# A graph network's row gathers: part of them issued row by row by SyncE and ScalarE instead of GpSimd

## The chip, the cores and the metric

The kernel runs on one core of a Trainium2 chip. The core has five engines with queues of their own: TensorE (PE, with its weight loads as PEld), VectorE (DVE), ScalarE (ACT), GpSimd (POOL) and SyncE (SP), and 16 DMA engines that all of them use. The metric is the time of one execution on the device, in microseconds (us).

## The reference, cut to what matters

Two graph layers on 12500 nodes of 128 numbers and 400000 edges sorted by destination. The change touches the first, a relational layer that is applied twice. Its core is a gather, a scaling and a sum by destination:

```
h   = relu(layernorm(x))
rel = argmax(edge_attr[:, 16:26])                  # relation of each edge, 0..9
seg = dst * 10 + rel
mean[seg] = sum over its edges of h[src] / count(seg)
h   = relu(einsum('nrd,rdo->no', mean, w_rel1) + h @ root1 + b1)
y   = the same once more with w_rel2, root2, b2;  x = x + y
```

The second layer is graph attention (xl[src], xr[dst], a softmax over the edges of a node, a weighted sum of xl[src]); the change leaves it alone.

## The kernel before, in words

The relational layer is turned round: for every node n and relation r the product h[n] @ w_rel[r] is made first and stored in DRAM as a table (`ytab` for the first pass, `ytab2` for the second). It has a row of 128 floats, 512 bytes, for each of the keys src*10 + rel. A pass then fetches for every edge the row of its key, scales it by 1/count, and sums rows by destination.

The 400000 edges are 3125 tiles of 128. Five tiles are a group (G = 5), five groups are a round (SLOTS = 5), so a pass has 625 groups and 125 rounds. I call the work on one group a slot.

- GpSimd (`gather_engine`) issues one indirect DMA a tile (L714), which fetches 128 rows by 128 keys. Five buffers `p_g` of a group each and five key buffers `p_i` go round. Before it refills one it waits until ScalarE has scaled the group five slots back (`s_free`, which is `s_v`).
- ScalarE (`rgcn_pass`) waits for the gather of a group, copies the keys of the group five slots ahead into `p_i` (L755), reads one number from a table into a register (`load`, L114), and scales the five tiles into a ring `p_v` of ten groups (L761).
- VectorE builds a 0/1 matrix from the destinations (L616) and adds each product to the node sums `A` (L635). TensorE multiplies the two (L678), five products a step.
- From group 500 or so on, the same loops also make the next table, node tile by node tile: for the second pass in pass 1 (`NextTable`), the attention's `xlw` and `xrw` in pass 2 (`Attention`). SyncE moves those tiles (its `sync` methods). Until then SyncE has nothing to do in a pass.

The prologue makes keys, counts and the first table. What sets the order is written out by hand: each engine has its own program, and semaphores tie them together.

In a row of the profile, L114 stands for the helper `load`, which reads numbers from SBUF into registers (TENSOR_LOAD), and L110 for the helper `gate`, which waits. Tile names lose their pass number: `p_g` is p1_g or p2_g.

Of the kernel before, what the change touches and what calls it, by code (L numbers as in the profile page):

```python
# [20 lines left out]
I32 = mybir.dt.int32  # L21
ALU = mybir.AluOpType
ACT = mybir.ActivationFunctionType
AX = mybir.AxisListType.X
ds = bass.ds

P = 128
N = 12500
D = 128
# [8 lines left out]
G = 5  # L38
# [18 lines left out]
LOOK = 6  # L57
ROUNDS = GROUPS // SLOTS
# [25 lines left out]
assert all(BLOCK * (NBLK - 2) + OUT_AT[b] >= GROUPS + OB * b + OB - 1 for b in range(OUTS))  # L84
assert AHEAD == UNROLL and NT % 2 == 0 and STEPS + UNROLL <= SCOLS * P
# [3 lines left out]
def build(nc, x, src, dst, attr, w_rel1, root1, b1, w_rel2, root2, b2, w_l, w_r, att, bias, out,  # L89
# [3 lines left out]
    def sem(name):  # L93
        return outer.enter_context(nc.semaphore(name))
# [50 lines left out]
    src_dram = nc.dram_tensor("src_dram", (P, CE), I32, kind="Internal").ap()  # L145
    xjw = nc.dram_tensor("xjw", (GROUPS + 1, P, GW), F32, kind="Internal").ap()

    with outer:
# [20 lines left out]
        def prologue():  # L169

            with ExitStack() as st:
# [24 lines left out]
                junk = rel_all[:, 0:GROUPS]  # L196
                ones = sbuf(st, "ones", [1, P])
# [23 lines left out]
                s_ea = [sem(f"ea_in{k}") for k in range(2)]  # L221
                s_dst, s_src, s_nb = sem("dst_in"), sem("src_in"), sem("neighbours_in")
                s_last, s_rel, s_iota = sem("last_in"), sem("ea_used"), sem("iotas")
                s_const, s_raw = sem("prep_const"), sem("raw_free")
                s_tp, s_ev = sem("turned"), sem("to_turn")
                s_pa, s_tz, s_key = sem("psum_free_act"), sem("turned_early"), sem("keys")
                s_tw, s_inv, s_wa = sem("turned_weights"), sem("inverse_counts"), sem("weights_copied")
                s_tab, s_step = sem("tables_made"), sem("tables_moved")
                s_eps, s_w = sem("t1_eps_set"), sem("t1_w_in")
                s_x = [sem(f"t1_x_in{k}") for k in range(2)]  # L230
                s_st, s_var, s_std, s_rs = sem("t1_stats"), sem("t1_variance"), sem("t1_std"), sem("t1_rstd")
                s_hn, s_t, s_ht = sem("t1_rows"), sem("t1_turned"), sem("t1_copied")
                s_m0, s_m1, s_y0, s_y1 = sem("t1_product0"), sem("t1_product1"), sem("t1_out0"), sem("t1_out1")
                s_out = [sem(f"t1_stored{k}") for k in range(2)]
                NB = NT // BT

                with nc.Block() as block:

                    @block.sync
                    def _(sp):  # L240
# [28 lines left out]
                        sp.dma_start(base[:, :], base_dram.rearrange("(a s) -> a s", a=1).to_broadcast([P, SCOLS * P])).then_inc(s_step, 16)  # L269
                        for k in range(2):  # L270
                            sp.wait_ge(s_out[k], 16 * (NT // 2))
                        sp.dma_start(steps[:, :], step_dram[0].rearrange("(a s) k -> a (s k)", a=1)).then_inc(s_step, 16)
                        sp.wait_ge(s_step, 192)
# [14 lines left out]
                    def _(dve):  # L288
# [111 lines left out]
                        v.engine_nop().then_inc(s_key, 1)  # L400
                        link(v.memset(tot, 1.0))
# [194 lines left out]
        def sum_engines(block, name, onehot, colsp, pg, V, width, s_v, s_pe, s_acc, then, localise=False):  # L596

            s_dl, s_oh = sem(f"{name}_local"), sem(f"{name}_onehot")
            s_cp = sem(f"{name}_cols_set")
# [100 lines left out]
        def gather_engine(block, rows, stage, gbuf, s_stage, s_g, s_free, s_kept=None):  # L700

            @block.gpsimd
            def _(pool):
                def round_(i, peel):
                    for k in range(SLOTS):
                        if peel:
                            pool.wait_ge(s_stage, k + 1)
                        else:

                            gate(pool, "pool", (s_free, SLOTS * (i - 1) + k + 1))  # L710
                            if s_kept is not None:
                                gate(pool, "pool", (s_kept[k], 16 * i))
# [999 lines left out]
```

## Time and profile before

| | us |
|---|---|
| runs on the device, median of 3 (lowest, highest) | 12650.64 (12648.94, 12654.09) |
| profiled execution: its own time is its span | 12683.4 |
| prologue, 0 to 680 | 680 |
| pass 1, first to last gather | 3907.5 |
| between the passes | 37 |
| pass 2, first to last gather | 3908 |
| change-over and attention | 4150 |

Busy shares over the whole span (the page's first part): PE 57%, DVE 42%, ACT 33%, POOL 71%. These are averages over stages that differ, so the stage of the two passes has to be read by itself. [...]

### The profile page before, as it was taken

To read this page: it belongs to the slowest core of one execution; us is meant where nothing else is said; L and a number is where in the kernel's file an instruction comes from. 1 tells how busy PE (TensorE), PEld (TensorE's weight loads), DVE (VectorE), ACT (ScalarE), POOL (GpSimd) and SP (SyncE) were. 2 spreads that over 40 slices of the span, in tenths; PEclk is the share of its full clock that TensorE was granted. 3 is DMA by queue.
4 is the path that set the end of the run, shared out by engine and by line. 5 is a ranking of instruction groups with operands and counts; after the bars stand their busy time and mean duration, and the time that the engine had idled before them with its cause. 6 is when DMAs were issued, how large, how long until landed. Compare 5 with 4: busy or idle time off the path is not lost. (4 is left out here: it accounts for less than half of the span.)

```text
span 12683.4 us, 185431 instructions
## 1 busy us (share of the span) xinstructions
PE 7179.3 (57%) x34895; PEld 6004.9 (47%) x34896; DVE 5378.0 (42%) x11674; ACT 4188.5 (33%) x12473; POOL 9042.4 (71%) x9581
## 2 busy tenths in 40 slices
PE   3744444444444864444444444556777877777777
PEld 1333333333333543333333343444666766666666
DVE  7832222222222641111111111353776766776767
ACT  2522222222222222222222222223444444444442
POOL 0167777777777767777777777767777777777776
PEclk8855555555555975555555555667998898998988
DMA  8622221122122542111222122236888888888887
GB/s 239 204 59 52 52 52 53 52 53 52 53 52 59 185 137 53 52 53 52 53 52 53 52 53 52 73 88 172 236 237 234 237 236 236 235 236 235 236 235 207
DMA packets 922670, 1589.56 MB, mean 125 GB/s; under 512 B 303128, under 2 KB 487318, under 8 KB 915334
## 3 DMA queue, kind: packets, MB, share of 16 engines
q0 software_dynamic: 314112, 685.63, 21.9%
q1 hardware_dynamic: 384568, 595.99, 15.3%
q10 hardware_dynamic: 223412, 301.41, 7.7%
q8 instruction: 219, 3.59, 0.1%
q14 instruction: 359, 2.94, 0.1%
HBM read 1213.18 MB, written 367.39 MB: 125 GB/s over the span
## 5 line engine op out<-in xcount | busy, mean ns | idle before, releaser
L714 POOL DMA_INDIRECT p_g<-ytab,p_i x6250 | 5912.3, 946 | 1973.2 <-issue 1661.9
L1165 POOL DMA_INDIRECT a_g<-xlw,a_i x3125 | 2986.1, 956 | 995.5 <-issue 875.4
L678 PE MATMUL p_pg<-p_v,p_oh 128*128 x6120 | 1338.9, 397 | 1550.0 <-ACT p_v L761 1549.4
L761 ACT ACTIVATE p_v<-p_g,wgt_all 128x128 f32<-128x128 f32 x6250 | 1960.4, 389 | 542.1 <-issue 517.0
L678 PEld LDWEIGHTS p_pg<-p_v,p_oh 128*128 128x128 f32 x6120 | 1200.0, 295 | 1710.1 <-issue 1699.5
L755 ACT ACTIVATE p_i<-rel_all 128x5 int32 (+1 forms) x1250 | 260.0, 208 | 5065.5 <-DMA p_g<-ytab,p_i 5065.5
L678 PE MATMUL p_pt<-p_v,p_oh 128*128 x4200 | 978.1, 416 | 1277.7 <-ACT p_v L761 1277.7
L678 PEld LDWEIGHTS p_pt<-p_v,p_oh 128*128 128x128 f32 x4200 | 876.4, 313 | 1376.5 <-issue 1376.5
L616 DVE TENSOR_TENSOR p_oh<-p_cols,local 128x640 f32<-128x640 f32 x1460 | 1196.1, 820 | 24.9
L1636 PE MATMUL a_px<-a_g,ident 128*128 x1450 | 740.7, 597 | 761.7 <-SPq L1219 673.0
L1625 PE MATMUL a_pg<-a_v,a_into 128*128 128x132 f32 x7000 | 984.2, 291 | 121.2 <-DVE A L1550 43.8
L635 DVE TENSOR_TENSOR A<-p_pg,A 128x128 f32 x612 | 178.0, 291 | 1978.6 <-PE p_pg L678 1977.3
L1625 PEld LDWEIGHTS a_pg<-a_v,a_into 128*128 128x128 f32 x7000 | 910.6, 203 | 139.2 <-issue 95.7
L1268 ACT ACTIVATE a_away<-a_dst,a_minus 128x640 f32 x727 | 602.8, 829 | 970.8 <-issue 385.3
L678 PE MATMUL y_py<-p_v,p_oh 128*128 x2080 | 494.2, 423 | 649.8 <-ACT p_v L761 649.8
L635 DVE TENSOR_TENSOR A<-p_pt,A 128x128 f32 x420 | 122.6, 292 | 1677.3 <-PE p_pt L678 1677.2
L1321 ACT ACTIVATE a_relu<-a_px 128x384 f32<-128x384 f32 x725 | 351.9, 485 | 1300.5 <-PE a_py L1642 1270.6
L678 PEld LDWEIGHTS y_py<-p_v,p_oh 128*128 128x128 f32 x2080 | 441.6, 318 | 700.2 <-issue 699.5
L1642 PEld LDWEIGHTS a_px<-a_xr,a_onto 128*128 128x128 f32 x4350 | 708.9, 220 | 69.0
L1642 PE MATMUL a_px<-a_xr,a_onto 128*128 128x132 f32 x4350 | 705.4, 306 | 0.0
L1559 DVE TENSOR_TENSOR a_relu<-a_relu,a_pcon 128x640 f32<-128x640 f32 x725 | 587.9, 811 | 274.1 <-ACT a_relu L1322 273.2
L1636 PEld LDWEIGHTS a_px<-a_g,ident 128*128 128x128 f32 x1450 | 243.0, 210 | 839.7 <-issue 838.6
(254 smaller groups left out, 9818.0 us busy)
## 6 DMA issues: line engine op xcount, KB each, us to landing
a_xj<-xjw ACTq DMA_DIRECT2D x725, 330.0 KB
xjw<-a_g SPq DMA_DIRECT2D x625, 330.0 KB
a_dst<-in_dst_dram SPq DMA_DIRECT2D x625, 320.0 KB
p_g<-ytab,p_i POOLq DMA_INDIRECT x6250
ytab<-steps POOLq DMA_DIRECT2D x98, 640.0 KB, 3.6
ytab<-src_i SPq DMA_DIRECT2D x98, 640.0 KB
ea<-in_edge_attr_dram SPq DMA_DIRECT2D x50, 1176.0 KB
a_g<-xlw,a_i POOLq DMA_INDIRECT x3125
```

The costliest lines, as they stand in the source:

```text
L616: v.tensor_tensor(onehot[k][:, :].rearrange("p (t n) -> p t n", t=G), colsp[:, 0:P].rearrange("p (a n) -> p a n", a=1).to_broadcast([P, G, ...
L635: v.tensor_tensor(A[:, ds(to[k], width)], pg[b][:, 0:width], A[:, ds(to[k], width)], ALU.add).then_inc(s_acc, 1)
L678: last = t.matmul(pg[b][:, 0:width], onehot[(at + k) % LOOK][:, q * P:(q + 1) * P], V[:, ds(to + q * width, width)], start=(q == 0), stop= ...
L714: pool.indirect_dma_start(gbuf[k][:, q * D:(q + 1) * D], None, rows, bass.IndirectOffsetOnAxis(ap=stage[k][:, q:q + 1], axis=0)).then_inc( ...
L761: last = a.activation(V[:, c:c + D], gbuf[k][:, q * D:(q + 1) * D], ACT.Copy, scale=wgt[:, ds(G * g + q, 1)])
L1165: pool.indirect_dma_start(gbuf[k][:, q * W:(q + 1) * W], None, xlw, bass.IndirectOffsetOnAxis(ap=stage[k][:, q:q + 1], axis=0)).then_inc(s ...
L1268: a.activation(away[:, :], dall[:, ds(at, GE)], ACT.Abs, bias=minus[:, ds(s, 1)]).then_inc(s_away, 1)
L1321: a.activation(lk[:, 0:HEADT, :], x3[:, :, 0:D], ACT.Relu)
L1559: v.tensor_tensor(lk, lk, attp.rearrange("p (a d) -> p a d", a=1).to_broadcast([P, G, D]), ALU.mult).then_inc(s_wt, 1)
L1625: last = t.matmul(sums(j, b), into[b][:, q * P:(q + 1) * P], V[b][:, q * W:(q + 1) * W], start=(q == 0), stop=(q == G - 1))
L1636: t.matmul(px[b], ident[:, :], gath[:, ds(ring, HEADT * W)], start=True, stop=False)
L1642: last = t.matmul(to, onto[b][:, q * P:(q + 1) * P], xr[k % RING][:, :], start=False, stop=q in (HEADT - 1, G - 1))
```

## The change

In each turn of ten rounds, the last tile of the last group of a round is no longer fetched by GpSimd in nine of the ten rounds. SyncE fetches it in rounds 1, 3, 5, 6 and 8 of turns 0 to 9, ScalarE in rounds 2, 4, 7 and 9 of all turns (12.5 turns a pass; the last has rounds 0 to 4). That is 50 + 50 tiles a pass, 200 of 6250 in all.

Such a tile is fetched as 128 transfers of one row. The keys, times 512, are made once in the prologue (`row_keys`). The engine fetches a line of 128 of them to SBUF, reads them into registers (16 at a time on SyncE, 4 on ScalarE), and issues one DMA of 512 bytes for each into a row of its own buffer (`p_spr`, `p_acr`), five and four buffers. ScalarE does so in pieces of four rows (I call one a chunk), 64 chunks in each five rounds, spread over the first 22 of their 25 slots, up to three after the scaling of a slot. SyncE does whole tiles, one after the other. When the tile is due, ScalarE waits for its 128 rows and scales them in place of the gathered ones.

Besides, the gather loop and ScalarE's loop now hold ten rounds in their bodies (before: one and two), and the semaphores of a phase are cleared and freed at its end, with a barrier of all engines (`clear_spent`, three times). A part of what SyncE did at the start of `sync` is now called ahead of its tiles (`sync_first`).

```
+TURN = 10
+FULL_TURNS = 10
+SP_ROUNDS = (1, 3, 5, 6, 8)
+ACT_ROUNDS = (2, 4, 7, 9)
+SP_BUFS, ACT_BUFS = 5, 4
+ROW = D * 4
+KEYS = (NT * P * NREL - 1) * ROW
+LOADED = 16
...
+ACT_SHARES = [[] for _ in range(TURN * SLOTS)]
+for _h in range(2):
+    _own = [m for m in range(len(ACT_ROUNDS)) if TURN // 2 * _h <= ACT_ROUNDS[m] < TURN // 2 * (_h + 1)]
+    _parts = [(m, c) for m in _own for c in range(0, P, 4)]
+    for _i, _part in enumerate(_parts):
+        ACT_SHARES[TURN // 2 * SLOTS * _h + _i * 22 // len(_parts)].append(_part)
...
+    def clear_spent():
+
+        nc.clear_and_free_semaphores(list(spent))
+        spent.clear()
+        nc.all_engine_barrier()
 
...
+                        sp.dma_start(row_keys, rk[:, :]).then_inc(s_step, 16)
...
+                        v.tensor_scalar(rk[:, :], key[:, CE - P:CE], float(ROW), None, ALU.mult).then_inc(s_rk, 1)
...
+        def by_rows(turn, r):
+
+            full = not isinstance(turn, int) or turn < FULL_TURNS
+            if full and r in SP_ROUNDS:
+                m = SP_ROUNDS.index(r)
+                return "sp", m % SP_BUFS, len(SP_ROUNDS) // SP_BUFS * turn + (m // SP_BUFS + 1)
+            if r in ACT_ROUNDS:
+                m = ACT_ROUNDS.index(r)
+                return "act", m % ACT_BUFS, len(ACT_ROUNDS) // ACT_BUFS * turn + (m // ACT_BUFS + 1)
+            return None
+
...
+        def gather_engine(block, rows, stage, gbuf, s_stage, s_g, s_free):
 
             @block.gpsimd
...
+                def body(turn):
+                    for r in range(rounds_in(turn)):
+                        for k in range(SLOTS):
+                            if isinstance(turn, int) and turn == 0 and r == 0:
+                                pool.wait_ge(s_stage, k + 1)
+                            else:
+
+                                gate(pool, "pool", (s_free, TURN * SLOTS * turn + (SLOTS * (r - 1) + k + 1)))
+                            for q in range(G):
+                                if k == SLOTS - 1 and q == G - 1 and by_rows(turn, r) is not None:
+                                    continue
+                                pool.indirect_dma_start(
+                                    gbuf[k][:, q * D:(q + 1) * D], None, rows,
...
+                        def keys(turn, m):
+
+                            sp.dma_start(spidx[m % SP_BUFS][:, :], row_keys[ds(TURN * turn + SP_ROUNDS[m], 1), :]).then_inc(s_spi[m % SP_BUFS], 16)
+
+                        def tile(turn, m, again):
+                            b, n = m % SP_BUFS, len(SP_ROUNDS)
+                            fills = n // SP_BUFS
+                            gate(sp, "sp", (s_spi[b], 16 * fills * turn + 16 * (m // SP_BUFS + 1)))
+                            if m >= SP_BUFS:
+                                gate(sp, "sp", (s_v, TURN * SLOTS * turn + SLOTS * (SP_ROUNDS[m - SP_BUFS] + 1)))
+                            elif not (isinstance(turn, int) and turn == 0):
+                                gate(sp, "sp", (s_v, TURN * SLOTS * turn + SLOTS * (SP_ROUNDS[m - SP_BUFS] + 1 - TURN)))
+                            for c in range(0, P, LOADED):
+                                at = load(sp, SP_, spidx[b], c, LOADED, KEYS)
+                                for e in range(LOADED):
+                                    sp.dma_start(sprow[b][c + e:c + e + 1, :].bitcast(U8),
+                                                 octets[ds(at[e], ROW)].rearrange("(a d) -> a d", a=1)).then_inc(s_spr[b], 16)
+                            if m + SP_BUFS < n:
+                                keys(turn, m + SP_BUFS)
+                            elif again:
+                                keys(turn + 1, m + SP_BUFS - n)
...
+                        then.sync_first(sp)
+                        for m in range(SP_BUFS):
+                            keys(0, m)
+                        for m in range(len(SP_ROUNDS)):
+                            tile(0, m, True)
+                        with sp.Fori(1, FULL_TURNS - 1) as turn:
+                            for m in range(len(SP_ROUNDS)):
+                                tile(turn, m, True)
+                        for m in range(len(SP_ROUNDS)):
+                            tile(FULL_TURNS - 1, m, False)
                         then.sync(sp)
 
                     @block.scalar
...
+                        def some_rows(turn, m, c):
+
+                            b = m % ACT_BUFS
+                            if c == 0:
+                                gate(act, "act", (s_aci[b], 16 * fills * turn + 16 * (m // ACT_BUFS + 1)))
+                                if m >= ACT_BUFS:
+                                    gate(act, "act", (s_v, TURN * SLOTS * turn + SLOTS * (ACT_ROUNDS[m - ACT_BUFS] + 1)))
+                                elif not (isinstance(turn, int) and turn == 0):
+                                    gate(act, "act", (s_v, TURN * SLOTS * turn + SLOTS * (ACT_ROUNDS[m - ACT_BUFS] + 1 - TURN)))
+                            at = load(act, ACT_, actidx[b], c, 4, KEYS)
+                            for e in range(4):
+                                act.dma_start(actrow[b][c + e:c + e + 1, :].bitcast(U8),
+                                              octets[ds(at[e], ROW)].rearrange("(a d) -> a d", a=1)).then_inc(s_acr[b], 16)
+                            if c + 4 == P:
+                                if m + ACT_BUFS < n:
+                                    if not (isinstance(turn, int) and TURN * turn + ACT_ROUNDS[m + ACT_BUFS] >= ROUNDS):
+                                        keys(turn, m + ACT_BUFS)
+                                elif not (isinstance(turn, int) and TURN * (turn + 1) + ACT_ROUNDS[m + ACT_BUFS - n] >= ROUNDS):
+                                    keys(turn + 1, m + ACT_BUFS - n)
+
...
+                        def body(turn):
+                            last = rounds_in(turn)
+                            for x in range(last * SLOTS):
+                                r, k = x // SLOTS, x % SLOTS
+                                g = TURN * SLOTS * turn + x
+                                gate(act, "act", (s_g[k], 16 * gathered(turn, r, k)))
 
...
-                        for i in range(ROUNDS // parts * parts, ROUNDS):
-                            round_(i, i % parts, False)
+                                    c = (x % VSLOTS * G + q) * D
+                                    rows = gbuf[k][:, q * D:(q + 1) * D]
+                                    single = by_rows(turn, r) if k == SLOTS - 1 and q == G - 1 else None
+                                    if single is not None:
+                                        who, b, filled = single
+                                        gate(act, "act", ((s_spr if who == "sp" else s_acr)[b], 16 * P * filled))
+                                        rows = (sprow if who == "sp" else actrow)[b][:, :]
+                                    to_v = a.activation(V[:, c:c + D], rows, ACT.Copy, scale=wgt[:, ds(G * g + q, 1)])
+                                to_v.then_inc(s_v, 1)
+                                for m, c in shares[x]:
+                                    if ACT_ROUNDS[m] < last:
+                                        some_rows(turn, m, c)
+                        for m in range(min(ACT_BUFS, n)):
+                            keys(0, m)
+                        turns(act, body)
 
         def tile_of(i, k, lag):
```

How the instructions move. GpSimd, pass 1, end of the round loop before (`p1_g4<-ytab,p1_i4` is a gather into buffer 4 with key buffer 4, `x5` five of them; REGISTER_ALU goes with a gate):

```order
L714 DMA p1_g2<-ytab,p1_i2 128x128 x5
L109 REGISTER_ALU
L714 DMA p1_g3<-ytab,p1_i3 128x128 x5
L109 REGISTER_ALU
L714 DMA p1_g4<-ytab,p1_i4 128x128 x5
L718 REGISTER_ALU
L718 COMPARE_AND_BRANCH
```

and the same place, now inside a body of ten rounds:

```order
L782 DMA p1_g2<-ytab,p1_i2 128x128 x5
L138 REGISTER_ALU
L782 DMA p1_g3<-ytab,p1_i3 128x128 x5
L138 REGISTER_ALU
L782 DMA p1_g4<-ytab,p1_i4 128x128 x4
L138 REGISTER_ALU
L782 DMA p1_g0<-ytab,p1_i0 128x128 x5
```

The last group of this round has four gathers instead of five, and the next round follows without a branch.

ScalarE, pass 1, in the loop, before (ISA is a register operation that an instruction needs; `p1_v<-p1_g1` scales a tile of group buffer 1):

```order
L761 ACTIVATE p1_v<-p1_g1,wgt_all 128x128
L761 ISA
L761 ACTIVATE p1_v<-p1_g1,wgt_all 128x128
L755 ISA
L755 ACTIVATE p1_i2<-rel_all 128x5
L114 ISA
```

and now, at the same slot of a round in which it issues rows (`p1_aci1` are the keys of a row tile, `p1_acr1` its buffer):

```order
L901 ACTIVATE p1_v<-p1_g1,wgt_all 128x128
L901 ISA
L901 ACTIVATE p1_v<-p1_g1,wgt_all 128x128
L143 TENSOR_LOAD p1_aci1
L873 DMA p1_acr1<-ytab 1x512 x4
L143 TENSOR_LOAD p1_aci1
L873 DMA p1_acr1<-ytab 1x512 x4
L143 TENSOR_LOAD p1_aci1
L873 DMA p1_acr1<-ytab 1x512 x4
L889 ISA
L889 ACTIVATE p1_i2<-rel_all 128x5
```

Between the scaling of a slot and the key copy of the next stand three register loads and twelve transfers.

SyncE, start of pass 1, before (`y2_b` and `y2_x` are the bias and node rows for the second table):

```order
L865 DMA y2_w<-in_L0_gnn_w_rel2_dram 128x10x128
L867 DMA y2_w<-in_L0_gnn_root2_dram 128x128
L868 DMA y2_b<-in_L0_gnn_b2_dram 1x128
L871 DMA y2_x0<-in_x_dram 128x128
L871 DMA y2_x1<-in_x_dram 128x128
L878 UNCONDITIONAL_BRANCH
```

and now, up to the first rows of its first tile:

```order
L1002 DMA y2_w<-in_L0_gnn_w_rel2_dram 128x10x128
L1004 DMA y2_w<-in_L0_gnn_root2_dram 128x128
L1005 DMA y2_b<-in_L0_gnn_b2_dram 1x128
L818 DMA p1_spi0<-row_keys 1x128
L818 DMA p1_spi1<-row_keys 1x128
L818 DMA p1_spi2<-row_keys 1x128
L818 DMA p1_spi3<-row_keys 1x128
L818 DMA p1_spi4<-row_keys 1x128
L143 TENSOR_LOAD p1_spi0
L831 DMA p1_spr0<-ytab 1x512 x16
L143 TENSOR_LOAD p1_spi0
L831 DMA p1_spr0<-ytab 1x512 x16
```

The loads of `y2_x` have moved behind all of SyncE's 50 tiles, and each 16 rows have one register load ahead of them.

## Rows read from the trace of the kernel before

**Rows 1.** By stage: pass 1, pass 2, attention; busy us of each engine
```profile
core 0: us, PE busy (x) PEld busy (x) DVE busy (x) ACT busy (x) POOL busy (x), PEclk, DMA share, GB/s
680.50:4588.00 3907.50, 1882.40 (x8018) 1569.18 (x8019) 1116.20 (x2716) 1107.53 (x3744) 2954.91 (x3124) 0.59 0.25 69
4625.00:8533.00 3908.00, 1752.81 (x7473) 1552.81 (x7474) 905.27 (x2281) 1107.49 (x3744) 2955.36 (x3125) 0.55 0.22 57
8890.00:12683.00 3793.00, 2918.31 (x17402) 2516.95 (x17401) 2654.52 (x5332) 1595.60 (x4169) 2838.56 (x2974) 0.90 0.83 233
```

**Rows 2.** Line L714, pass 1: durations in ns, then what ended POOL's idle time
```profile
L714 POOL DMA_INDIRECT p_g<-ytab,p_i x3125: 941/947/1037, 680.5 to 4588.0; - x196
  issue: 839.2, 2752
  ACT p_v L761: 113.4, 372
```

**Rows 3.** Longest waits, 1000 to 3000 us: total us, times, longest
```profile
ACT p_i L755 <- DMA p_g<-ytab,p_i: 1292.8, 320, 4.2
POOL p_g L714 <- issue: 419.6, 1376, 0.3
```

**Rows 4.** Timeline of ScalarE, one slot of pass 1
```profile
2001.61 0.21 ACT L755 ACTIVATE p_i<-rel_all 128x5 int32 x1 [4.00 <-DMA p_g<-ytab,p_i]
2002.26 1.57 ACT L761 ACTIVATE p_v<-p_g,wgt_all 128x128 f32<-128x128 f32 x5 [0.44 <-issue]
```

**Rows 5.** Waits of SyncE's queue over the whole span: total us, times, longest
```profile
SPq L110 <- DVE A L824: 3801.6, 96, 3423.1
```

**Rows 6.** Line L761 in one slot: ScalarE's register operations, ns, first and last start
```profile
L761 ACTq FUSED_REGOPS  x5: 43/46/46, 2002.2 to 2002.6; - x5
```

**Rows 7.** Timeline of ScalarE, attention: a transfer issued ahead of queued operations
```profile
9013.13 0.34 ACTq L1280 DMA_DIRECT2D a_xj<-xjw  x1
9013.36 0.76 ACT L1273 ACTIVATE a_onto<-a_away 128x640 f32<-128x640 f32 x1
```

**Rows 8.** Line L114 on ScalarE, register loads of one value
```profile
L114 ACTq TENSOR_LOAD <-done x320: 273/278/291, 1001.1 to 2996.1; - x160
```

**Rows 9.** Line L114 on VectorE: pass 1, then pass 2
```profile
L114 DVEq TENSOR_LOAD <-steps x462: 300/310/359, 1000.0 to 2995.0; - x154
...
L114 DVEq TENSOR_LOAD <-steps x92: 339/344/353, 5025.7 to 6996.2; - x92
```

**Rows 10.** Timeline of SyncE at pass 1's start: transfers issued
```profile
680.16 0.64 SPq L867 DMA_DIRECT2D y_w<-in_L_gnn_root_dram  x1
680.85 0.28 SPq L868 DMA_DIRECT2D y_b<-in_L_gnn_b_dram  x1
681.17 0.82 SPq L871 DMA_DIRECT2D y_x<-in_x_dram  x2
```

**Rows 11.** Timeline of SyncE: four transfers one behind the other, two places
```profile
4629.06 1.72 SPq L1019 DMA_DIRECT2D xl_heads<-in_L_gnn_att_dram  x4
...
8577.70 1.79 SPq L1192 DMA_DIRECT2D a_dst<-in_dst_dram  x4
```

**Rows 12.** Line L1276, ScalarE's transfers with an address from a register, ns
```profile
L1276 ACTq DMA_DIRECT2D a_xr<-xrw x728: 338/339/2139, 8580.3 to 12529.0; - x182
```

**Rows 13.** Line L1149 on VectorE, branch back of a long loop
```profile
L1149 DVEq COMPARE_BRANCH  x1: 74/74/74, 9270.4 to 9270.4; - x1
L1149 DVEq FUSED_REGOPS  x1: 98/98/98, 9273.7 to 9273.7; - x1
```

**Rows 14.** Line L718 on GpSimd, branch back of the gather loop, round 1
```profile
L718 POOLq COMPARE_BRANCH  x1: 50/50/50, 727.9 to 727.9; - x1
```

**Rows 15.** Timeline of GpSimd at the start of pass 2
```profile
4624.85 0.94 POOL L714 DMA_INDIRECT p_g<-ytab,p_i  x1 [35.88 <-ACT p_i L748]
```

**Rows 16.** Stage 4200 to 4588 us, columns as in rows 1
```profile
4200.00:4588.00 388.00, 328.02 (x1375) 197.81 (x1376) 242.17 (x648) 110.31 (x373) 293.22 (x310) 0.94 0.57 187
```

**Rows 17.** Page, part 5: attention's gathers, busy us, mean ns, idle us before
```profile
L1165 POOL DMA_INDIRECT a_g<-xlw,a_i x3125 | 2986.1, 956 | 995.5 <-issue 875.4
```

More of the change, by code:

```diff
@@ L219, in prologue @@
                 early = [range(q, min(q + 4, CT)) for q in range(0, CT, 4)]
[L221 to L232, printed above, removed]
@@ new lines, in prologue @@
+                s_pa, s_tz, s_key = sem("psum_free_act", True), sem("turned_early", True), sem("keys", True)
+                s_tw, s_inv, s_wa = sem("turned_weights", True), sem("inverse_counts", True), sem("weights_copied", True)
+                s_tab, s_step = sem("tables_made", True), sem("tables_moved", True)
+                s_eps, s_w = sem("t1_eps_set", True), sem("t1_w_in", True)
+                s_x = [sem(f"t1_x_in{k}", True) for k in range(2)]
+                s_st, s_var, s_std, s_rs = sem("t1_stats", True), sem("t1_variance", True), sem("t1_std", True), sem("t1_rstd", True)
@@ new lines, in gathered, with turns @@
+        def gathered(turn, r, k):
+            if k < SLOTS - 1:
+                return G * TURN * turn + G * (r + 1)
+            at = [G - (by_rows(0, n) is not None) for n in range(TURN)]
+            if not isinstance(turn, int) or turn < FULL_TURNS:
+                return sum(at) * turn + sum(at[0:r + 1])
+            late = [G - (by_rows(FULL_TURNS, n) is not None) for n in range(TURN)]
+            return sum(at) * FULL_TURNS + sum(late) * (turn - FULL_TURNS) + sum(late[0:r + 1])
+        def turns(eng, body):
+            body(0)
+            with eng.Fori(1, FULL_TURNS) as turn:
+                body(turn)
+            for turn in range(FULL_TURNS, -(-ROUNDS // TURN)):
+                body(turn)
@@ L702, in _, with rounds_in @@
+        def rounds_in(turn):
+            return min(TURN, ROUNDS - TURN * turn) if isinstance(turn, int) else TURN
+        def gather_engine(block, rows, stage, gbuf, s_stage, s_g, s_free):
             @block.gpsimd
             def _(pool):
[L704 to L712, printed above, removed]
-                        for q in range(G):
-                            pool.indirect_dma_start(
-                                gbuf[k][:, q * D:(q + 1) * D], None, rows,
-                                bass.IndirectOffsetOnAxis(ap=stage[k][:, q:q + 1], axis=0)).then_inc(s_g[k], 16)
@@ L722, in rgcn_pass @@
+                turns(pool, body)
         def rgcn_pass(name, first, table, following):
@@ L748, in _, with keys @@
                             a.activation(stage[k][:, :], rel_i[:, k * G:(k + 1) * G], ACT.Copy).then_inc(s_stage, 1)
-                        def round_(i, part, peel):
-                            for k in range(SLOTS):
-                                g = SLOTS * i + k
-                                gate(act, "act", (s_g[k], 16 * G * (i + 1)))
+                        n = len(ACT_ROUNDS)
+                        fills = n // ACT_BUFS
+                        shares = ACT_SHARES
+                        def keys(turn, m):
+                            act.dma_start(actidx[m % ACT_BUFS][:, :], row_keys[ds(TURN * turn + ACT_ROUNDS[m], 1), :]).then_inc(s_aci[m % ACT_BUFS], 16)
```

94 lines of the change are left out of this document (56 added, 38 removed).

## The prediction

> **What bounds the kernel now.** I read the stages first. The two relational passes take 3907.5 and 3908 us, and in both GpSimd is the busiest engine by far: 2955 us, against 1882 for TensorE, 1116 for VectorE and 1107 for ScalarE [rows 1]. That is 76%, not 100%, so the next question is what GpSimd does in the rest. Its 3125 gathers of a pass take 947 ns each, and the idle time ahead of them is about 0.30 us every time (839.2 us over 2752, 113.4 over 372), whether "issue" or ScalarE is named as what ended it [rows 2]. A wait that is always 0.30 us is no wait. It belongs to the instruction: first to last start is 3907.5 us for 3124 steps, 1.251 us a gather, with no hole anywhere. GpSimd is the bound of both passes from end to end. The other side of it: of the 320 slots between 1000 and 3000 us, ScalarE waited in every one for the gather to land, 1292.8 us in all, 4.0 us a slot of 6.25 [rows 3, 4]. SyncE's longest wait is 3423 us, since it has nothing to do in most of a pass [rows 5]. So there is spare sequencer time on both engines that get the new work, and every gather taken from GpSimd is worth 1.251 us as long as GpSimd stays the bound.
>
> **What is removed.** 50 + 50 tiles a pass, 200 of 6250: 200 x 1.251 = 250.2 us. Ten rounds fall from 312.7 to 241 x 1.251 = 301.4 us, five rounds from 156.3 to 150.7 on average. The new work must fit below these.
>
> **ScalarE's new work.** What a slot costs its sequencer now: from the key copy to the first scaling 0.65 us [rows 4], then five scalings at 0.10 us each, as its register operations from 2002.2 to 2002.6 show [rows 6], and 0.15 for waits ahead: 1.3 us. The scalings run for 1.57 us, but the sequencer doesn't wait for them: in the attention a transfer starts at 9013.13 although an operation that stands ahead of it in the program starts only at 9013.36 [rows 7]. So transfers are issued beside the scalings. 25 slots are 32.5 us.
>
> A chunk is one register load of four values and four transfers. The load: 278 ns for one value on ScalarE [rows 8]; on VectorE loads that are mostly of one value take 310, loads of four 344 [rows 9], so 11 ns a further value: 0.31, and with 0.04 to the next instruction 0.35 us. A transfer of one row of 512 bytes issued from a register's address isn't in the trace. From below: `y_b`, exactly one row of 512 bytes into one partition, 0.28 us and 0.04 to the next start, right behind other transfers [rows 10]. From above: 128-partition transfers in a chain (1.79 for four, so (1.79 - 0.43)/3 = 0.45) and those of 32 partitions (1.72 for four, 0.43) [rows 11]. Between them 128 partitions with an address from a register, 0.34, with the same gap 0.38 to 0.39 [rows 12]. I take 0.32, since y_b has the size and the shape. A chunk is then 0.35 + 4 x 0.32 = 1.63 us, 64 of them in five rounds 104.3, and with the slots 136.8 us, below 150.7. ScalarE stays hidden with 14 us to spare. Three chunks (4.9 us) can delay the key copy of a gather that has landed; five buffers are 30 us of distance, so GpSimd doesn't see it. ScalarE becomes the bound when a row costs more than (150.7 - 32.5 - 64 x 0.35)/256 = 0.374 us, and all gain is gone at about 0.394.
>
> **SyncE's new work.** A tile is 8 loads of 16 values (0.28 + 15 x 0.011 + 0.04 = 0.49), 3.9 us, 128 rows at 0.32, 41.0, and its keys and waits 0.5: 45.4 us. Five are 227 us of 301. It would bind from a row of 0.43 us. In turn 0 the first tile is due after ten slots, about 61 us, and ready after 50. In pass 2 SyncE first waits for small weight loads issued until 4630.8 [rows 11]; the tile is then there at about 4681, and due at 4686. The node rows that SyncE used to fetch at once it now fetches after 50 tiles, some 3000 us into the pass; they are first used after 3400 us [rows 5]. Both cost nothing. If that cover were gone, a late tile would cost its lateness once, since the next ones are made faster than they are used.
>
> **The longer loop bodies.** A long body has a price at its branch: VectorE's loop in the attention branches at 9270.4 and has its next instruction at 9273.7, 3.3 us [rows 13]. GpSimd's short loop branches without loss. Its body is now ten times as long, and it branches 16 times in all: 53 us if it were exposed. But GpSimd's sequencer runs ahead: it branches at the end of round 1 at 727.9 [rows 14], while by 1.251 us a gather that round's last one ends at 680.5 + 50 x 1.251 = 743. Fifteen microseconds of issued gathers cover 3.3. I take 0, with 53 as the other end. [...]
>
> **Small terms.** Three clears with a barrier: the change-over that is there cost 35.9 us of idle, nearly all of it work that drains [rows 15], so a barrier by itself is a few tenths; I take 5 us in all (0 to 12). Three more start-up operations (key table, key lines): 3 us. In the stretch where the next table is made TensorE is busy 328 of 388 us at a clock of 0.94 [rows 16]; there only ScalarE's tiles are gone (20 of the 200, 25 us), and I let 10 of it be lost (0 to 25). More DMA traffic could stretch a gather: with DMA engines busy 83% it comes to (2986.1 + 995.5)/3125 = 1.274 us [rows 1, 17]. The rows add 13 MB to 410, but 25,600 transfers; of the upper end, 5950 x 0.023 = 137 us, I take 8, near the level of the passes.
>
> **Sum.** -250.2 + 5 + 3 + 10 + 8 = -224 us. The profiled execution would go from 12,683 to 12,459. The runs' median lies 33 us (0.26%) under the profiled one; the same difference from it gives 12,427 us.
>
> **Rivals.** First, a row costs 0.39, as an address from a register did on 128 partitions [rows 12]. ScalarE then needs 32.5 + 22.4 + 256 x 0.39 = 154.7 us for five rounds and becomes the bound; 50 such halves save 1.6 us each, 80 in all, less 26: 12,597. For it: the address does come from a register. Against: fixed addresses on as many partitions are no cheaper (0.43 in a chain), so the register seems free.
>
> Second, the slower side: rows in a long chain cost what the chains of four did, 0.42 to 0.45 [rows 11]. ScalarE needs 162.4 to 170.1 us in place of 156.3, in each of 50 halves: +305 to +690, and 26: 12,980 to 13,370. It decides from 0.394 on. For it: the second to fourth of a chain cost 0.1 more than the first, and here chains are endless, and two engines feed the same DMA engines, a row every 0.26 us. Against: y_b stood in a chain too and cost 0.28.
>
> [...]
>
> Fourth, GpSimd's freed time turns into a wait. ScalarE is the one that releases buffers and now is 90% taken, so GpSimd waits for a buffer, or TensorE at half clock can't go faster (1882 busy of 3907 us speaks against [rows 1]). Then 12,650 to 12,680.
>
> **How the numbers follow.** Forecast 0.67, its own range 12,395 (nothing of the small terms) to 12,520 (branches and some stretching of the gathers exposed). First rival 0.12, second 0.12, third 0.04, fourth 0.05. What a measurement of this kernel can tell from no change is 0.2%, 25 us, so 12,625 to 12,676. Faster: 0.67 and most of the first rival, 0.76. Same: the rest of the first and half of the fourth, 0.05. Slower: 0.19. The range 12,395 to 12,660 leaves out the second and third rival and a little at the low end.
>
> **What would show it.** In the profile after: gathers of L782 at 1.25 us without holes, 5950 of them, a pass of about 3785 us; ScalarE still waiting 1 to 2 us a slot for them; row transfers on SPq and ACTq of about 0.28 us, register loads of 0.31 and about 0.45. If rows are 0.38 or more, or GpSimd shows waits for ScalarE's `p_v` of microseconds and no longer 0.30, the forecast is wrong by its row price. If ScalarE waits for `p_spr`, SyncE was too slow; holes of 3 us once in ten rounds would be the branches.

## The result: 5.4% slower, and ScalarE is the bound

The changed kernel takes 13,342.97 us (median of 4 runs, 13,275.6 to 13,409.0) against 12,649.79 us before on the same chip (12,644.9 to 12,654.1): ratio 1.0544, 95% interval 1.0506 to 1.0581. The forecast was 12,427, the range 12,395 to 12,660; both are missed, on the slower side. The profiled execution has a span of 13,407.1 us, 723.7 above the one of before, and is the slowest of the four: their spread is 1%, where the kernel before has 0.07%. Its stages and sums are read from that execution, and so lie a little above the median.

The stages come first (columns as in [rows 1]: PE, PEld, DVE, ACT, POOL busy, clock, DMA share, GB/s; pass 1, pass 2, attention). This is the changed kernel:

```profile
673.70:4961.30 4287.60, 1848.47 (x7935) 1549.09 (x7935) 1097.72 (x2678) 1087.95 (x3720) 2854.27 (x3025) 0.59 0.23 63
5017.40:9239.40 4222.00, 1682.14 (x7413) 1501.68 (x7413) 891.86 (x2231) 1087.35 (x3724) 2855.00 (x3025) 0.56 0.21 54
9590.00:13407.00 3817.00, 2935.83 (x17512) 2536.57 (x17512) 2668.47 (x5360) 1603.87 (x4190) 2856.34 (x2994) 0.90 0.83 234
```

Pass 1 is 380 us longer and pass 2 314; what is left of the 724 is 19 between the passes (56.1 us from the last gather of pass 1 to the first of pass 2, against 37), 18 behind pass 2 and 7 less in the prologue. GpSimd does 3025 gathers a pass and not 3125, exactly as meant, and is busy for 67% of it where it was 76%. It has lost work and takes longer: another engine holds it.

Which one, the gathers say. Line L782 of the changed kernel is L714 of before, whose idle time was 0.30 us a gather whatever was named [rows 2]:

```profile
L782 POOL DMA_INDIRECT p_g<-ytab,p_i x6050: 938/944/1075, 673.7 to 9238.4; - x196
...
  issue: 1699.9, 5433
  ACT p_v L901: 1100.3, 615
  ACT p_i L853: 89.0, 2
...
  ACT p_i L889: 84.8, 15
```

A gather lasts 944 ns, where it was 947. "issue" is still 0.31 us each, but 615 gathers waited 1.79 us on average for ScalarE's scaling `p_v`. The last line is the other side: ScalarE waited for a gather 15 times in the whole run, 84.8 us in all, where it had waited in every slot [rows 3]. These are its longest waits between 1000 and 3000 us, and then TensorE's:

```profile
ACT p_i L889 <- issue: 1334.8, 256, 5.9
ACT p_v L901 <- issue: 164.5, 254, 0.9
```

```profile
PE p_pg L713 <- ACT p_v L901: 424.1, 85, 6.8
PE y_py L713 <- ACT p_v L901: 418.3, 86, 6.6
```

ScalarE's compute unit is busy for 500 of these 2000 us. Of the rest it waits 1335 ahead of key copies and 165 ahead of scalings, all but 1 us of it for nothing but its own sequencer, which is issuing. A slot on its timeline (start, us, then the operation; [rows 4] is the same place before):

```profile
2001.70 0.98 ACT L901 ACTIVATE p_v<-p_g,wgt_all 128x128 f32<-128x128 f32 x3 [0.63 <-issue]
2002.57 0.47 ACTq L873 DMA_DIRECT2D p_acr<-ytab  x1
2002.59 0.68 ACT L901 ACTIVATE p_v<-p_g,wgt_all 128x128 f32<-128x128 f32 x2
2003.13 5.46 ACTq L873 DMA_DIRECT2D p_acr<-ytab  x11
2008.83 0.21 ACT L889 ACTIVATE p_i<-rel_all 128x5 int32 x1 [5.57 <-issue]
```

The first of the slot's three register loads starts at 2002.2. Twelve transfers, with the other two loads among them, take from 2002.57 to 2008.59; then the next key copy goes at once. From key copy to key copy the slot is 7.97 us, where GpSimd needs 6.25. The lines with ACTq are issues of transfers. None of their 6 us is counted as busy, yet the key copy behind them comes 5.57 us after the last scaling, and the trace names no wait.

What the order lists of ScalarE's scaling and key copy call ISA are the FUSED_REGOPS of the trace, register operations. In a slot of the kernel before, five of 43 to 46 ns go with the five scalings [rows 6], and one of 69 ns goes 0.1 us ahead of the key copy:

```profile
L755 ACTq FUSED_REGOPS  x1: 69/69/69, 2001.5 to 2001.5; - x1
L755 ACT ACTIVATE p_i<-rel_all x1: 209/209/209, 2001.6 to 2001.6; 128x5 int32 x1
```

GpSimd's new body has its branches back 350.2 us apart, 2028.7 and 2378.9 (rows in the section on the experiments), and none between: one in ten rounds.

**The price that was missed.** These are line L873 (ScalarE's row transfers), L831 (SyncE's) and L143 (register loads) over the whole run. The three numbers behind the colon are the shortest, the median and the longest duration in ns:

```profile
L873 ACTq MOVE p_acr<-ytab x12800: 29/29/38, 682.3 to 9249.7; - x197
L873 ACTq DMA_DIRECT2D p_acr<-ytab x12800: 228/229/961, 682.3 to 9249.8; - x197
```

```profile
L831 SPq DMA_DIRECT2D p_spr<-ytab x12800: 224/225/493, 679.8 to 8154.8; - x197
```

```profile
L143 ACTq TENSOR_LOAD <-p_aci x3200: 307/585/1363, 681.7 to 9247.9; - x189
...
L143 ACTq TENSOR_LOAD <-done x1230: 273/467/1228, 749.9 to 9251.8; - x176
...
L143 SPq TENSOR_LOAD <-p_spi x800: 1131/1230/1441, 678.5 to 8148.7; - x160
```

A row is cheap: 229 ns, 29 for its MOVE, 0.03 between each, 0.318 us from one to the next. But the load of four has its median at 585 ns and its minimum at 307, and the load of one value (`done`) went from 278 [rows 8] to 467; with no rows at all (e3) it is 278 again. Three windows around single instructions show what decides. First load of the slot, behind register operations of the scalings; the two other loads, behind transfers; the first four transfers:

```profile
L143 ACTq TENSOR_LOAD <-p_aci x1: 314/314/314, 2002.2 to 2002.2; - x1
```

```profile
L143 ACTq TENSOR_LOAD <-p_aci x2: 587/596/605, 2004.0 to 2006.4; - x2
```

```profile
L873 ACTq DMA_DIRECT2D p_acr<-ytab x4: 228/229/471, 2002.6 to 2003.8; - x4
```

A load right behind a transfer takes 0.27 us more (0.59 for 0.31), and the first transfer behind a load 0.23 to 0.27 more (0.46 to 0.50 for 0.229). I call it a change of kind when a register load follows a transfer or a transfer follows a load; on ScalarE each costs about a quarter of a microsecond. Why it does is not shown. A chunk is then 0.345 + 0.55 + 3 x 0.318 = 1.85 us as the first of its slot and 0.615 + 0.55 + 0.954 = 2.12 us behind another one; the prediction had 1.63.

### The profile page after: what moved, and what is told of

The parts are those of the page before. It is cut to its first block and busy times, and to the rows that moved or that the text cites. A ratio compares the mean times of both kernels' runs of the same rounds, so it can differ in the third digit from the quotient of the medians.

```text
span 13407.1 us, 238630 instructions
## 1 busy us (share of the span) xinstructions
PE 7092.9 (53%) x34895; PEld 5952.1 (44%) x34896; DVE 5371.6 (40%) x11675; ACT 4161.1 (31%) x12473; POOL 8838.0 (66%) x9381
## 5 line engine op out<-in xcount | busy, mean ns | idle before, releaser
L782 POOL DMA_INDIRECT p_g<-ytab,p_i x6050 | 5709.3, 944 | 2889.3 <-issue 1699.9
L901 ACT ACTIVATE p_v<-p_g,wgt_all 128x128 f32<-128x128 f32 x6050 | 1901.2, 388 | 660.5 <-issue 650.5
```

The source lines that it names most:

```text
L782: pool.indirect_dma_start(gbuf[k][:, q * D:(q + 1) * D], None, rows, bass.IndirectOffsetOnAxis(ap=stage[k][:, q:q + 1], axis=0)).then_inc( ...
L901: to_v = a.activation(V[:, c:c + D], rows, ACT.Copy, scale=wgt[:, ds(G * g + q, 1)])
```

## The experiments

Theory A is this price at the change of kind. Against it stood the prediction's rivals (rows in a long chain cost more; register loads cost by the value) and the structure around them (bodies of ten rounds, clears). Sixteen runs were made on four chips, four on each: A (e1 to e4), B (e5 to e8), C (e9 to e12) and D (e13 to e16). On B and C every kernel, the one before too, takes at least 23% longer than on A and D; their times get a part of their own. The changed kernel itself ran beside none of these; it is set against A and D because the kernel before agrees there to 0.04% with its time in the section on the result (12,655 and 12,654 for 12,650).

**Chip A (the kernel before there: 12,654.91 us).** The two halves of the change alone, then neither:

```
e1_sync_only:   ACT_ROUNDS = ()
e2_scalar_only: SP_ROUNDS = ()
e3_no_rows:     ACT_ROUNDS = (); SP_ROUNDS = ()
```

> ScalarE fetches no rows, SyncE its five tiles of ten rounds as in the change; all else as in the change. Theory A (ScalarE's instruction sequencer is the bound of the changed passes, since a register load behind transfers takes 0.59 us and the first transfer behind a load 0.46): GpSimd binds again, 100 gathers saved, 12,650 - 125 + 25 = about 12,550. Theory B (SyncE's part is what hurts: its tiles come late, or its transfers slow those of ScalarE): stays near 13,300. Theory C (the long loop bodies or the clears cost it): still over 12,900.

> SyncE fetches no rows, ScalarE its four tiles of ten rounds as in the change. Theory A: ScalarE binds just as before, ten rounds stay at 350 us, 13,340 (13,250 to 13,400). Theory B: SyncE gone, so about 12,550; if the two only disturb each other, row transfers and loads on ScalarE get shorter and the time falls to between. Theory C: as theory A in time, so e3 tells.

> No tile is fetched by rows: GpSimd gathers all 6250 as before the change, but with the loops of ten rounds, the key table, the clears with barriers. Theory A: 12,650 to 12,680 (the 16 branches of 2.6 us hidden by gathers issued ahead, clears some 5 us). Theory C: most of the +693 us is here, 13,000 and more.

| kernel | us | ratio, 95% interval |
|---|---|---|
| SyncE's tiles only | 12,537.13 | 0.9912, 0.9897 to 0.9927 |
| ScalarE's tiles only | 13,266.53 | 1.0477, 1.0446 to 1.0507 |
| no rows at all | 12,657.25 | 1.0004, 0.9995 to 1.0013 |

The structure costs nothing. SyncE's half gains 118 us: 100 gathers at 1.251 are 125. The loss is ScalarE's, and it is there with SyncE's transfers gone, so it is not, in the main, two engines' transfers that disturb each other. A disturbance of at most 76 us is left open: "ScalarE's tiles only" is that much faster than the changed kernel, though ScalarE does the same in both.

**Pieces of sixteen.** Same rows, same engine, a quarter of the changes of kind:

```
-    _parts = [(m, c) for m in _own for c in range(0, P, 4)]
+    _parts = [(m, c) for m in _own for c in range(0, P, 16)]
...
-  at = load(act, ACT_, actidx[b], c, 4, KEYS)
-  for e in range(4):
+  at = load(act, ACT_, actidx[b], c, 16, KEYS)
+  for e in range(16):
```

> The change with one edit: ScalarE loads 16 keys at a time and issues 16 transfers behind each load (8 pieces a tile, not 32 of four). Same rows, same transfers. Theory A: a quarter of the changes between load and transfer; a piece is 1.2 + 0.46 + 15 x 0.32 = 6.4 us, five rounds 16 x 6.4 + 25 x 1.9 = 150 us against 151 of GpSimd, so 12,430 to 12,550. Rival (the price is of the rows or of the values loaded, not of the change of instruction): 13,200 to 13,350.

12,417.05 us (12,405.4 to 12,424.2), ratio 0.9814 (0.9799 to 0.9829): 926 us off the changed kernel, faster than both kernels, 10 us from the forecast and 13 below the lower end of what was expected of this run. 12,800 row transfers on ScalarE are in it, so it is not their number or their chain that costs. Its gathers and its loads of sixteen:

```profile
L782 POOL DMA_INDIRECT p_g<-ytab,p_i x6050 | 5709.4, 944 | 1922.9 <-issue 1772.8
```

```profile
L143 ACTq TENSOR_LOAD <-p_aci x800: 1002/1024/2404, 683.8 to 8255.1; - x160
```

Idle time before gathers is 1922.9 us over 6050, 0.32 each: no holes, GpSimd binds again. The load of sixteen takes 1.02 us where four took 0.31, so a value above four costs 0.06 us, more than the 0.011 I had from VectorE's loads of one and four [rows 9], but 0.25 for four values is half of what the two changes of kind cost, 0.50.

**What the loads and transfers cost by themselves** (e5 and e7, on chip B, where times can't be set beside these; single instructions can, where none is delayed). e5 puts all loads of a slot ahead of all its transfers; e7 loads each key twice in a row, and the transfers of rows 1 and 2 take their addresses from the first load, 3 and 4 from the second:

```
e5:  now = [(m, c) for m, c in shares[x] if ACT_ROUNDS[m] < last]
     ats = [some_rows(turn, m, c) for m, c in now]     # the loads
     for (m, c), at in zip(now, ats):
         send_rows(turn, m, c, at)                     # the transfers
e7:  at = load(act, ACT_, actidx[b], c, 4, KEYS)
+    again = load(act, ACT_, actidx[b], c, 4, KEYS)
+    at = [at[0], at[1], again[2], again[3]]
```

> The change with one edit: behind the scalings of a slot ScalarE first makes all its register loads (two or three of four keys), then all its transfers. Same loads, same transfers, but one change from load to transfer and one back in a slot, not three. Theory A1 (the price sits at the change between the two kinds of instruction): a slot is 1.6 + 3 x 0.34 + 0.49 + 11 x 0.32 = 6.6 us, five rounds 152 to 154, just over GpSimd's 151, so 12,480 to 12,560. Theory A2 (each load costs 0.59 and makes 0.23 for itself wherever it stands): 13,250 to 13,350 as in the change.

> The change with each of ScalarE's key loads made twice, one behind the other; the first two rows use the first load's values, the last two the second's. Theory A1: the second load of a pair takes 0.31 us and the first transfer still 0.46, though its address has been there for a whole load: +22 us in five rounds, about 14,400. Theory A2: the second also takes 0.59, about 15,300. If the 0.46 were a wait for the register just loaded, the first transfer would take 0.23.

e7 (17,476.33 us, one run), the two loads of a chunk at 2007.2, then its four transfers:

```profile
L143 ACTq TENSOR_LOAD <-p_aci x2: 303/304/306, 2007.2 to 2007.5; - x2
```

```profile
L875 ACTq DMA_DIRECT2D p_acr<-ytab x4: 228/230/462, 2007.9 to 2009.1; - x4
```

The pair of the next chunk, behind these transfers:

```profile
L143 ACTq TENSOR_LOAD <-p_aci x2: 308/444/581, 2009.3 to 2010.0; - x2
```

A load behind a load costs 0.30; behind transfers the first of a pair takes 0.58 and the second 0.31 again. The first transfer still takes 0.46, though its address had been in its register for 0.3 us. So it isn't a wait for the register that the transfer uses, and the load as such isn't dear: the price is paid by the instruction that changes the kind. That speaks against a price by the value too: a load of four takes 0.30 here, where one value took 0.278 [rows 8].

**The same in times** (chip D: before 12,654.43 us). e13 is e5's kernel, e15 e8's with pieces of eight (8 in place of 4 in the diff of e4), e14 gives ScalarE `ACT_ROUNDS = (4, 9)` with `ACT_BUFS = 2`, two tiles of ten rounds in chunks of four; e16 is "no rows" again.

> All loads of a slot first, then all its transfers. Price at the change between load and transfer (theory A): five rounds 32.5 + 64 x 1.6 + 25 x 0.45 = 146 us on ScalarE, just below GpSimd's 150.7: 12,420 to 12,560 on a chip where the kernel before takes 12,650. A price for each transfer with an address from a register (theory B): 13,343, as with loads and transfers by turns. On a chip where the kernel before takes 15,600: 17,350 again.

> ScalarE fetches two tiles of ten rounds in chunks of four. Theory A: 32 chunks of some 2.0 us and the slots are 97 us in five rounds, hidden; 50 gathers less than with SyncE alone, 12,537 - 63 = 12,475. Something that doesn't grow with the number of chunks: above 12,537. On a chip where the kernel before takes 15,600: 17,980 again.

> Pieces of eight. Theory A: 32 pieces of 3.25 us in five rounds and the slots, 138 us, hidden: 12,417 to 12,450. Theory B: 13,343. On a chip where the kernel before takes 15,600: 18,240 again.

> The long loop bodies, clears and key table with no row fetched by SyncE or ScalarE. On a chip like the first: 12,657 again. [...]

| kernel | us | ratio, 95% interval |
|---|---|---|
| loads first | 12,447.82 | 0.983, 0.9813 to 0.9846 |
| half of the rows | 12,472.29 | 0.9855, 0.9839 to 0.9872 |
| pieces of eight | 12,500.36 | 0.9872, 0.9855 to 0.9889 |
| no rows | 12,654.67 | 1.0001, 0.9991 to 1.0011 |

"Loads first" differs from the changed kernel in nothing but the order inside a slot: as many loads, of as many values, as many transfers. It is 895 us faster, and its single loads take 307 ns in the median where they took 585. Together with e7 that shows the cause. "Half of the rows" came out 3 us from its number. "Pieces of eight" is 50 above its upper end: I had left out that ScalarE's slots are dearer as well (below). The expectation of e8 for the same kernel had them at 1.8 us, and its 12,450 to 12,560 holds the 12,500. In the stretch from 1000 to 3000 us ScalarE's loads in "loads first" are what A says, and with half of the rows it waits for the gathers again, 3.7 us a slot:

```profile
L143 ACTq TENSOR_LOAD <-p_aci x835: 302/307/327, 1005.8 to 2997.1; - x167
```

```profile
ACT p_i L889 <- DMA p_g<-ytab,p_i: 1207.2, 328, 4.5
```

**One price list for six kernels.** The list prices the instructions of ScalarE's sequencer for five rounds. A slot without chunks is taken as 1.63 us, from one slot: key copies of the changed kernel at 2048.51 and 2050.14, while ScalarE catches up.

```profile
2048.51 0.20 ACT L889 ACTIVATE p_i<-rel_all 128x5 int32 x1
2048.67 1.57 ACT L901 ACTIVATE p_v<-p_g,wgt_all 128x128 f32<-128x128 f32 x5
2050.14 0.19 ACT L889 ACTIVATE p_i<-rel_all 128x5 int32 x1
```

Five rounds have 25 slots, 40.8 us; in the 22 with chunks the `done` load stands behind transfers, 0.19 more each, 4.2; half of the branch's 2.6 is 1.3: 46.2 us. To it come the pieces, 22 of them first in their slot where there are as many. With pieces of sixteen only 16 slots have one, so the slots are 45.1 there. GpSimd's five rounds are 150.7 us with all nine tiles off, 151.9 in "half of the rows". "Measured" is half of a full turn of ten rounds in the middle of a pass; for the changed kernel it is the distance of GpSimd's branches back, 2028.7 and 2378.9:

```profile
L759 POOLq COMPARE_BRANCH  x2: 45/49/53, 2028.7 to 2378.9; - x2
L759 POOLq FUSED_REGOPS  x2: 49/49/49, 2031.3 to 2381.5; - x2
```

| kernel | pieces, us | with slots | GpSimd | measured |
|---|---|---|---|---|
| changed | 22 x 1.85 + 42 x 2.12 = 129.7 | 175.9 | 150.7 | 174 to 175.1 |
| loads first | 64 x 0.337 + 22 x 0.23 + 256 x 0.318 = 108.0 | 154.2 | 150.7 | 152.4 to 153.1 |
| pieces of eight | 22 x 3.36 + 10 x 3.64 = 110.3 | 156.5 | 150.7 | 155.5 |
| pieces of sixteen | 16 x 6.37 = 102.0 | 147.1 | 150.7 | 150.5 |
| half of the rows | 22 x 1.85 + 10 x 2.12 = 61.9 | 108.1 | 151.9 | 151.7 |
| ScalarE only | as changed | 175.9 | 153.9 | 171.3 to 173 |

(A piece of eight: load 0.553 and 0.03, first transfer 0.55, seven at 0.318; 0.28 more behind another piece. One of sixteen: 1.02 and 0.03, 0.55, fifteen.) The larger of the two sums is what was measured, to about 1%; with ScalarE alone it is 1.7 to 2.7% too high, and why is not shown.

**Two chips on which all is slower.** e5 to e8 ran on chip B (before: 15,606.11 us). Three of them ran again as e10 to e12, with e4's kernel beside them as a measure: e9 is e4's kernel, e10 e8's, e11 e5's, e12 e6's. They landed on chip C (before: 15,594.55 us). e6 is "half of the rows", e8 "pieces of eight".

> The change with ScalarE fetching two tiles in ten rounds (rounds 4 and 9), not four; SyncE five. Loads of four keys as in the change. Theory A: 32 chunks of about 2 us and 25 slots of 1.7 are 107 us in five rounds, GpSimd binds at 122 gathers, 150 gathers saved in all: 12,650 - 187 + 5 = about 12,465. If ScalarE's capacity isn't the point: over 12,600.

> The change with loads of 8 keys and 8 transfers behind each (16 pieces a tile). Theory A: a piece is about 0.55 + 0.06 + 0.49 + 7 x 0.32 = 3.3 us, 3.6 behind another piece; five rounds 22 x 3.3 + 10 x 3.6 + 25 x 1.8 = 154 us, just over GpSimd's 151: 12,450 to 12,560, between e4 and the change and near e4.

> The kernel of the pieces of sixteen once more, as the measure for the three beside it. Where the chip is like the one of the first four experiments: 12,417 us, 12,400 to 12,440. Where it is like the one of the second four, every kernel with row tiles is slower than the kernel before, and this one too; then the chip and not the piece's size made those four times.

> Pieces of eight. Theory A (price where loads and transfers alternate): a piece is 0.55 for its load, 0.46 for the first transfer and 7 x 0.32: 3.25 us, 32 of them in five rounds 104 us and the slots 32.5 and five or so prices of 0.28 where one piece follows another: about 138 us, below GpSimd's 150.7. 12,417 again, at most 12,450. Theory B (a price for each register that a transfer takes its address from, whatever the piece): as long as with pieces of four, 13,343.

> All loads of a slot first, then all its transfers. Theory A: a chunk is 0.315 + 4 x 0.32 = 1.60 and a slot pays one 0.23 at the first transfer and one 0.15 to 0.27 at the first load behind: five rounds 32.5 + 64 x 1.6 + 25 x 0.45 = 146 us, just below 150.7: 12,420 to 12,560. Theory B: as long as with loads and transfers by turns, 13,343.

> ScalarE fetches two tiles of ten rounds and not four, with the same chunks of four. Theory A: a five-round half with 32 chunks is 32.5 + 32 x 2.0 = 97 us, far below GpSimd's; 6250 - 300 = 5950 + 100 gathers... that is 100 gathers fewer taken off than in the changed kernel, 250 + 100 = 350 with SyncE's five of ten. In numbers: SyncE alone gave 12,537; two of ten rounds on ScalarE are 50 gathers over both passes, 50 x 1.251 = 62 us less: 12,475. Theory B (ScalarE's share hurts by something that doesn't grow with its chunks, such as the buffers' order): above 12,537.

| kernel | chip B: us, ratio | chip C: us, ratio | A or D: us |
|---|---|---|---|
| pieces of sixteen | - | 17,531.4, 1.1273 (1.1207 to 1.1338) | 12,417 |
| loads first | 17,388.04, 1.114 (1.1121 to 1.1159) | 17,341.95, 1.1109 (1.1089 to 1.113) | 12,448 |
| half of the rows | 17,980.33, 1.1526 (1.1507 to 1.1545) | 17,980.95, 1.1527 (1.1506 to 1.1549) | 12,472 |
| pieces of eight | 18,237.99, 1.1684 (1.1665 to 1.1704) | 18,239.62, 1.1694 (1.1675 to 1.1714) | 12,500 |

The times expected of a chip like A did not come there, for any of them, and e9 with the best kernel of chip A shows that the chip makes these times and not the size of the pieces. (e12's expectation has a slip in its middle; its number, 12,475, is the one that counts.) The same code on the two kinds of chip, first where it takes 12,417 us, then where it takes 17,531: sixteen row transfers of one piece, and SyncE's address moves between 3000 and 4000 us.

```profile
3003.62 5.25 ACTq L873 DMA_DIRECT2D p_acr<-ytab  x16
...
L831 SPq MOVE p_spr<-ytab x951: 29/29/37, 3000.0 to 3427.1; - x191
```

```profile
3004.39 12.47 ACTq L873 DMA_DIRECT2D p_acr<-ytab  x16
...
L831 SPq MOVE p_spr<-ytab x1355: 2/29/1410, 3000.0 to 3999.7; - x194
```

There is one such move ahead of each transfer; it takes 29 ns on the one chip and up to 1410 on the other, where some take 2, and the sixteen transfers take 12.47 us in place of 5.25. What makes them slow there is not shown: the run that was to tell whether it is the rows or the long bodies (e16, the bodies without rows) landed on chip D. The changed kernel was not run on B or C. The medians of B and C agree to 0.3%, so it is no scatter; and it has no part in the loss of 5.4%, where ScalarE's moves are 29 ns in the median and at most 38, SyncE's at most 43.

## Why the prediction was wrong

**The failed step is the chunk: "0.35 + 4 x 0.32 = 1.63 us".** It took the load and the row each from a place where the neighbour was of its own kind or a register operation: 278 ns among the scalings' register operations [rows 8], `y_b` behind another transfer [rows 10]. In the new code they alternate. Measured are 1.85 and 2.12 us; for five rounds 129.7 in place of 104.3, 25 us more: one or two changes of kind in every chunk, which the sum had at nothing. That alone would have gone past the 14 us to spare.

**The slots were undersized too: 1.3 us.** Without a chunk they are 1.63, with one 1.82, since the `done` load now stands behind transfers and pays the change as well. 46.2 in place of 32.5, 14 us more, just all of the slack. With the chunks right and the slots wrong, ScalarE would have been at the edge, as "loads first" is with 153.

Both together: 176 us in place of 136.8, against GpSimd's 150.7. Over by some 24.5 as measured, in each half of a full turn. The nine turns in the middle of both passes make 9 x 2 x 49 = 882 us of it, of the 916 between forecast and result.

**Which rival was right.** That ScalarE becomes the bound was the second rival's outcome, and 13,343 lies in its 12,980 to 13,370. Its mechanism is refuted: a row in a chain costs 0.318 on ScalarE, and on SyncE, at the same time, sixteen in a row take 5.06 us, 0.319 each. Its threshold, "from 0.394 on", was worked out with the chunk's other terms fixed, and those moved. The third rival (chance 0.04) was that register loads cost by the value. No run shows the price that it needed: here a load of four takes 0.307 us behind a load, of eight 0.553 and of sixteen 1.024, so a value above four is 0.06. The sign on record for this outcome, GpSimd waiting microseconds for `p_v`, did show; it was to mean a wrong row price, and the row price held. A number that fits is no proof of its story; the change of kind and the dear row both gave a time near 13,300, and only the single durations told them apart.

**What held.** The row at 0.32 (0.318). GpSimd's 1.251 us for each gather taken off: "SyncE's tiles only" gained 118 of 125 us, pieces of sixteen 238 of 250, so the small terms are 12 in place of 26: 12,417 against 12,427. SyncE stays hidden, though its price was low, 45.4 us predicted: a tile's transfers run for 50.96 us (row below) and with its first load 52.2; five are 261 of GpSimd's 301, and ScalarE has no wait for `p_spr`. Its loads of sixteen take 1.23 us and not 0.45.

```profile
2027.95 50.96 SPq L831 DMA_DIRECT2D p_spr<-ytab  x128
```

The branches too: GpSimd's body of ten rounds loses 2.6 us at its end (2028.7 to 2031.3, in the rows of the branches above), yet "no rows" costs 0 to 0.1%, so the run-ahead covers it as [rows 14] let expect. VectorE's 3.3 [rows 13] has its like there, hidden.

The chances were wrong where the slack was thin. ScalarE had 14 us of 150 to spare on an operation that no row of before showed in its new neighbourhood, and I gave 0.28 to its being the bound (the first three rivals), 0.16 of it to a loss. The prediction also counts 5950 gathers that are left, where there are 6050; only the 137 us of an upper end came from that.

## What to carry to other kernels

Price an instruction on a sequencer by its neighbour, not only by itself: here, on ScalarE, a register load behind a transfer cost 0.27 us more and a transfer behind a load 0.23 more, so many addresses should be loaded at once and the transfers issued in one run behind them (12,417 against 13,343 us for the same rows). An engine whose compute unit is idle 75% of the time can be full all the same, as ScalarE was here (busy for 500 of 2000 us); add up its sequencer, register operations and transfers included, and when the sum leaves a tenth to spare on prices never seen side by side, let the range reach to the other side. The sign that it still fits is in the profile: the engine that got the work still waits for the old bound, as ScalarE does with half of the rows.

## What the runs showed that I had not expected

- The change of kind on ScalarE: load of four 0.307 behind a load, 0.314 behind register operations, 0.585 behind a transfer; first transfer behind a load 0.46, any other 0.229. With the address in its register for 0.3 us already the first transfer still took 0.462 (e7).
- SyncE pays much less for it. Below are the transfers of one tile, eight of them behind a load, and the seven of its eight loads that stand behind transfers. No transfer takes over 289 ns, at most 0.06 us more than the median. The loads behind transfers take 1.23 us; the shortest load of the run takes 1.13, so my estimate for the change to a load is some 0.1.

```profile
L831 SPq DMA_DIRECT2D p_spr<-ytab x128: 224/225/289, 2028.0 to 2078.7; - x128
...
L143 SPq TENSOR_LOAD <-p_spi x7: 1227/1232/1239, 2033.0 to 2072.5; - x7
```

- A register load costs 0.06 us for each value above four on ScalarE (medians 0.307, 0.553 and 1.024 for 4, 8 and 16, in e13, e15 and e4), and 1.23 for sixteen on SyncE behind transfers.
- Chips differ: 12,650 and 15,600 us for the same kernel, and 12,417 and 17,531 for the best one, which is 1.9% faster than the kernel before on one kind and 12.7% slower on the other.
